# First cross attention of a six-stage kernel: output product from rounded parts and rests, and loads and first products in another order

## What is computed

```python
def _L0_xattn_ref(latents, context, ln_l_w, ln_l_b, ln_c_w, ln_c_b, Wq, Wkv, Wo, bo):
    H, D = 16, 64                    # INNER = 1024
    lat = layernorm(latents, ln_l_w, ln_l_b)
    ctx = layernorm(context, ln_c_w, ln_c_b)
    q = (lat @ Wq).reshape(b, n, H, D).transpose(0, 2, 1, 3)
    k, v = jnp.split(ctx @ Wkv, 2, axis=-1)
    ...
    attn = jnp.clip(jnp.einsum('bhnd,bhsd->bhns', q, k) * D ** (-0.5), -11.0, 11.0)
    attn = jax.nn.softmax(attn, axis=-1)
    out = jnp.einsum('bhns,bhsd->bhnd', attn, v)
    return out.transpose(0, 2, 1, 3).reshape(b, n, INNER) @ Wo + bo

x = x + _L0_xattn_ref(_layernorm(x, axis=-1), ctx_1024, ...)     # x (16, 64, 256), ctx (16, 256, 256)
x = x + _L0_attn_ref(_layernorm(x, axis=-1), ...)                # and four stages more
```

## Time and profile before

| | us |
|---|---|
| median of 3 runs | 1001.87 |
| lowest, highest | 1000.32, 1002.91 |
| the profiled execution | 1002.35 |
| its span, first to last instruction | 1000.6 |
| TensorE busy in the span | 953.0 (95%) |
| VectorE, ScalarE, GpSimd busy | 612.9, 446.0, 169.0 |
| mean granted clock of TensorE | 0.986 of 2.4 GHz |

### The profile page before, as it was taken

The page is one execution under the profiler, slowest core; times in us unless marked ns, Lnnn a source line. Parts: engine busy times, 40 slices in busy tenths (PEclk is TensorE's granted clock), DMA queues, the critical chain, the costliest instruction groups (busy, mean ns, idle before and its releaser), DMA issues.

```text
span 1000.6 us, 25932 instructions
## 1 busy us (share of the span) xinstructions
PE 953.0 (95%) x10693; PEld 818.4 (82%) x10693; DVE 612.9 (61%) x1448; ACT 446.0 (45%) x893; POOL 169.0 (17%) x357
## 2 busy tenths in 40 slices
PE   5999999999999989999989999997999999999998
PEld 4788888888888777887779999995888887877887
DVE  5655754654532655667798787776787863554242
ACT  3333332333332466654236666653444343673241
POOL 2312212112012212334310000013112000110000
PEclk9999999999999999999999999997999999999999
DMA  9443142132110292000059999962312002000000
GB/s 323 129 106 75 33 106 74 33 85 52 35 40 4 80 382 85 3 12 24 23 157 343 377 356 360 307 131 46 54 35 44 3 3 75 3 2 1 11 11 22
DMA packets 158612, 101.16 MB, mean 101 GB/s; under 512 B 102104, under 2 KB 148128, under 8 KB 157984
## 3 DMA queue, kind: packets, MB, share of 16 engines
q1 hardware_dynamic: 156960, 95.31, 31.9%
q0 software_dynamic: 1536, 4.20, 1.3%
HBM read 82.96 MB, written 16.52 MB: 99 GB/s over the span
## 4 chain that ended last, share of the span: by engine, by line
PE 82%; DVE 9%; ACT 5%; issue 2%; DMA 1%; POOL 0%; SPq 0%; DVEq 0%; ACTq 0%; POOLq 0%
PE ps L642 9%; PE ps L657 8%; PE ps L2374 8%; PE ps L2387 6%; PE ps L2710 6%; PE ps L674 3%; PE ps L1488 3%; PE ps L1195 3%; PE ps L596 3%; PE ps L693 2%; PE ps L1585 2%; PE ps L626 2%; PE ps L1120 2%; PE ps L1527 2%; PE ps L1130 2%; PE ps L1569 2%
## 5 line engine op out<-in xcount | busy, mean ns | idle before, releaser
L2374 PE MATMUL ps<-moe_xT,ew 128*128 128x128 f32 x736 | 89.5, 275 | 0.9 <-issue 0.8
L785 ACT ACTIVATE x0pT<-ps 128x512 f32<-128x512 f32 x64 | 38.2, 598 | 110.9 <-PE ps L657 110.9
L2374 PEld LDWEIGHTS ps<-moe_xT,ew 128*128 128x128 f32 x736 | 85.8, 192 | 1.7 <-issue 1.4
L1029 POOL TENSOR_SCALAR x0pT<-x0pT 128x512 f32<-128x512 f32 x64 | 40.3, 630 | 188.1 <-ACT x0pT L785 187.1
L2710 PE MATMUL ps<-f,ffw 128*128 128x512 f32 x256 | 60.7, 398 | 0.8 <-issue 0.6
L2710 PEld LDWEIGHTS ps<-f,ffw 128*128 128x128 f32 x256 | 48.9, 192 | 12.0 <-issue 0.9
L2387 PE MATMUL ps<-ew_2hi,eh_hi 128*128 128x256 f32 x184 | 55.5, 301 | 3.2 <-DVE eh_lo L2513 2.8
L642 PE MATMUL ps<-x0wv_hi,x0cT_hi 128*128 128x512 f32 x128 | 53.2, 416 | 4.2 <-DVE x0A_lo L915 4.2
L2323 DVE TENSOR_TENSOR ew_2lo<-ew,ew_2hi 128x1024 fp32r<-128x1024 f32 x46 | 55.9, 1216 | 0.0
L2570 POOL DMA_INDIRECT yg<-moe_out,slot x16 | 16.3, 1017 | 232.2 <-DMA moe_out<-moe_y 162.1
L657 PE MATMUL ps<-x0A_hi,x0cT_hi 128*128 128x512 f32 x128 | 52.0, 406 | 2.5 <-ACT x0pT L785 2.5
(11 more groups left out here) (337 smaller groups left out, 2428.7 us busy)
## 6 DMA issues: line engine op xcount, KB each, us to landing
ew<-L_ffn_W_dram SPq DMA_DIRECT2D x46, 1024.0 KB, 7.7
x0cin<-ctx_dram SPq DMA_DIRECT2D x8, 512.0 KB, 4.7
x1cin<-ctx_dram SPq DMA_DIRECT2D x64, 64.0 KB
x0cn_rows<-x0cn SPq DMA_DIRECT2D x7, 512.0 KB, 2.8
x0cn_blocks<-x0cn_rows SPq DMA_DIRECT2D x56, 64.0 KB, 2.4
x0att_rows<-x0att SPq DMA_DIRECT2D x14, 256.0 KB, 2.5
x0att_blocks<-x0att_rows SPq DMA_DIRECT2D x56, 64.0 KB, 2.6
moe_out<-moe_y SPq DMA_DIRECT2D x23, 128.0 KB, 4.3
```

What stands on the lines that cost most here:

```text
L785: nc.scalar.activation(g.pT[:, u, :], ps[:, S_BANK[u % 2], :], ACT.Exp, scale=64.0 ** -0.5).then_inc(C0.exp, 1)
L1029: nc.gpsimd.tensor_scalar(g.pT[:, u, :], g.pT[:, u, :], high, low, ALU.min, ALU.max).then_inc(C0.clip, 1)
L2374: last = nc.tensor.matmul(ps[:, n % 3, j * BT:j * BT + BT], ew1[b % NW][:, i, f * P:f * P + P], xT[b % 2][:, i, :], start=(i == 0), stop=( ...
```

## The change

*Output product.* `wo` is split once, in tile 0, into `wo_hi` (ScalarE, into the room of `w_sq[0]`) and `wo_lo` (VectorE, in place). The attention rows of each tile are split into `attT_hi` (ScalarE, into the second half of `padneg`) and `attT_lo` (VectorE, in place). A product of 8 float32 steps becomes one of 24 fp32r steps. It stands behind the eighth score group of the next tile, not between score groups 3 and 4; that of tile 6 stands in the next stage's list. `padneg` is set to zero again by GpSimd when x is done.

*Start.* TensorE begins with 18 products of zeros, then turns the K weights, then the latents, then the context. The latents are normalised ahead of the context rows. SP loads only the identity's 128 columns of the constants at first.

*Tile 0.* Turning the context of tile 1 moves behind v7 on VectorE and its scaling behind the last exponential on ScalarE.

*Loads.* The weights of the self attention and `wg` are loaded behind tile 0's attention rows, those of `w_sq[0]` when x is done.

The diff, cut to its core:

```diff
-        def ln_rstd_pool(pool, k, idx):
+        def ln_rstd_pool(pool, k, idx, first=0):
+            c = slice(first, first + k)
...
-            FILLS += [(("x0", t - 1), "y")] * (t > 0) + [(("x0", t + 1), "lat")] * nxt
-            FILLS += [(("x0", t), f"v{i}") for i in range(4, 8)]
+            FILLS += [(("x0", t + 1), "lat")] * nxt
+            FILLS += [(("x0", t), f"v{i}") for i in range(4, 8)] + [(("x0", t - 1), "y")] * (0 < t < T - 1)
             if nxt:
...
+            def out_products(t, what, ks):
+                for k in ks:
+                    for n, (m, w) in enumerate(((g.attT_hi, g.wo_hi), (g.attT_hi, g.wo_lo), (g.attT_lo, g.wo_hi))):
+                        last = nc.tensor.matmul(bank_of(t, what)[:, 0:D], m[:, k, :], w[:, k, :], start=(k == ks[0] and n == 0), stop=(k == ks[-1] and n == 2))
+                last.then_inc(C0.fill, 1)
+
             def fill_y(t):
...
-                pe.wait_ge(C0.attT, 2 * t + 2)
+                    pe.wait_ge(C0.w_lo, KD + 4)
...
+            pe.wait_ge(C0.zeros_lat_ones, 1)
+            for _ in range(18):
+                nc.tensor.matmul(ps[:, S_BANK[0], 0:P], g.pT[:, 0, 0:P], g.pT[:, 0, 0:P], start=True, stop=True, skip_group_check=True)
+            pe.wait_ge(ld["const"], 32)
+            for i in range(4):
+                fill_K(i)
+            fill_lat(0)
             fill_cT(0, 0)
...
-                if t > 0:
-                    fill_y(t - 1)
                 if nxt:
...
+                if 0 < t < T - 1:
+                    fill_y(t - 1)
...
+            def attT_upper(t):
+                act.wait_ge(C0.attT, 4 * t + 2)
+                if t > 0:
+                    wait_filled(act, t - 1, "y")
+                for pg in range(2):
+                    nc.scalar.activation(g.attT_hi[:, 4 * pg:4 * pg + 4, :], g.attT[:, 4 * pg:4 * pg + 4, :], ACT.Copy).then_inc(C0.attT_hi, 1)
+
+            def attT_upper_last(pg):
+                wait_filled(act, T - 1, f"T{pg}")
+                nc.scalar.activation(g.attT_hi[:, 4 * pg:4 * pg + 4, :], bank_of(T - 1, f"T{pg}").rearrange("p (c n) -> p c n", c=4), ACT.Copy).then_inc(C0.attT_hi, 1)
+
+            def wo_upper(i):
+                if i == 0:
+                    act.wait_ge(ld["x0o"], 16)
+                nc.scalar.activation(g.wo_hi[:, 2 * i:2 * i + 2, :], g.wo[:, 2 * i:2 * i + 2, :], ACT.Copy).then_inc(C0.w_hi, 1)
...
+            K(0)
+            K(1)
+            K(2)
+            lat(0)
             cT(0)
-            K(0)
-            lat(0)
-            K(2)
...
+                if nxt and t > 0:
+                    cT(t + 1)
                 if nxt:
-                    cT(t + 1)
...
+                if t > 0:
+                    attT_upper(t - 1)
+                if t == 0:
+                    wo_upper(0)
+                    wo_upper(1)
                 v(t, 6)
                 exp(t, 6)
                 exp(t, 7)
+                if t == 0:
+                    cT(1)
+                    wo_upper(2)
+                    wo_upper(3)
...
+            def attT_lower(t, pg):
+                dve.wait_ge(C0.attT_hi, 2 * t + pg + 1)
+                half = slice(4 * pg, 4 * pg + 4)
+                nc.vector.tensor_tensor(g.attT_lo[:, half, :], g.attT[:, half, :], g.attT_hi[:, half, :].bitcast(F32), ALU.subtract).then_inc(C0.attT, 1)
...
+            def norm_first():
+                dve.wait_ge(ln_rstd, 1)
+                nc.vector.tensor_scalar(g.lat[:, :], x[:, 0, :], ln_mv[:, 4, 0:1], ln_rs[:, 4:5], ALU.subtract, ALU.mult).then_inc(C0.zeros_lat_ones, 1)
+                dve.sem_inc(dve_go, 1)
+                dve.wait_ge(C0.zeros_lat_ones, 2)
+                nc.vector.bn_stats(g.ln_st[:, 4, :], g.lat[:, :]).then_inc(ln_stats, 1)
+                dve.wait_ge(ln_stats, 2)
+                dve.sem_inc(dve_go, 1)
+                nc.vector.bn_aggr(ln_mv[:, 4, :], g.ln_st[:, 4, :]).then_inc(ln_aggr, 1)
+                for k in range(4):
+                    last = nc.vector.tensor_scalar(g.cn[:, k, :], g.cin[:, 0, k, :], ln_mv[:, k, 0:1], ln_rs[:, k:k + 1], ALU.subtract, ALU.mult)
+                last.then_inc(ln_done, 1)
+                dve.wait_ge(ln_rstd, 2)
+                nc.vector.tensor_scalar(g.lat[:, :], g.lat[:, :], ln_mv[:, 4, 0:1], ln_rs[:, 4:5], ALU.subtract, ALU.mult).then_inc(ln_done, 1)
+
+            nc.vector.memset(g.pT[:, 0, 0:P], 0.0).then_inc(C0.zeros_lat_ones, 1)
...
-                if nxt:
+                if nxt and t > 0:
                     turn_context(t + 1)
+                if t > 0:
+                    v(t, 3)
+                if nxt and t > 0:
+                    cT(t + 1)
+                    cT_split(t + 1)
+                if more:
+                    norm(t + 2, 1)
                 if t > 0:
                     turn_att(t - 1, 0)
                     turn_att(t - 1, 1)
-                    v(t, 3)
-                if nxt:
-                    cT(t + 1)
-                    cT_split(t + 1)
-                if t > 0:
-                    residual(t - 1)
-                if more:
-                    norm(t + 2, 1)
                 v(t, 5)
                 if more:
                     norm(t + 2, 2)
+                if t > 0:
+                    attT_lower(t - 1, 0)
+                    attT_lower(t - 1, 1)
                 v(t, 7)
+                if 0 < t < T - 1:
+                    residual(t - 1)
                 if more:
                     norm(t + 2, 3)
+                if t == 0:
+                    turn_context(1)
+                    cT(1)
+                    wo_lower(0)
                 attend(t, 0)
+                if t == 0:
+                    cT_split(1)
                 if nxt:
                     q(t + 1)
+                if t == 0:
+                    wo_lower(1)
+                    wo_lower(2)
+                    wo_lower(3)
+                if nxt:
                     A_lower(t + 1, 0)
                     A_lower(t + 1, 1)
                     attend(t, 1)
@@ -1018,7 +1093,7 @@
                     v(t + 1, 1)
                 if t == 1:
                     self_tables(dve)
-            return attend, attT, add_y, residual
+            return attend, attT_lower_last, add_y, residual
 
         def pool_x0(pool):
...
+                x0_y(T - 2)
...
+                x0_residual(T - 2)
+                x0_attT(0)
...
-            whole(cst[:, :], a["consts"], ld["const"])
+            whole(ident, a["consts"][:, C_IDENT:C_IDENT + P], ld["const"])
...
+            whole(cst[:, P:C_ALL], a["consts"][:, P:C_ALL], ld["rest"])
...
+                if t == 2:
+                    for i, w in enumerate(("wq", "wkv")):
+                        whole(w_mla[:, :, 64 * i:64 * i + 64], weight("L0_attn_" + w), ld["mla"])
+                    for i, w in enumerate(("wqr", "wqr_swapped", "wkr", "wkr_swapped")):
+                        whole(w_mla[:, :, P + P * i:2 * P + P * i], weight("L0_attn_" + w), ld["mla"])
+                    whole(w_mlao[:, :, :], weight("L0_attn_wo"), ld["mla"])
+                    sp.wait_ge(pool_setup, 4)
+                    whole(w_mlac[0:64, 0:P], a["L0_attn_wqc"], ld["mla"])
+                    whole(w_mlac[64:P, P:2 * P], a["L0_attn_wkc"], ld["mla"])
+                    whole(w_mlac[64:P, 2 * P:2 * P + D], a["L0_attn_wv"], ld["mla"])
+                    whole(wg[:, :, 0:E], weight("L0_ffn_Wg"), ld["wg"])
             sp.wait_ge(C0.x_done, T)
+            for i, w in enumerate(("Wq", "Wk", "Wv", "Wo")):
+                whole(w_sq[0][:, :, i, :], weight("L0_ffn_" + w), ld["sq0"])
             for i, w in enumerate("QKVO"):
...
+            nc.gpsimd.memset(padneg[:, B // 2:B, :], 0.0).then_inc(pool_setup, 1)
```

More of the change, by code:

```diff
@@ L1857, in act_self @@
                 hT(lo)
-                last(T - 1)
+                last(0)
                 lat(lo)
@@ L1861, in act_self @@
                 rope(lo)
+                last(1)
                 hT(lo + 1)
@@ L2969, in _ @@
         def _(pe):
-            pe.wait_ge(ld["const"], 32)
             x0 = pe_x0(pe)
```

107 lines of the change are left out of this document (48 added, 59 removed).

## The result

| kernel | median us | lowest to highest | executions |
|---|---|---|---|
| before | 1001.10 | 1000.30 to 1002.91 | 4 |
| after | 989.05 | 986.92 to 989.54 | 4 |

The medians differ by 12.05 us, 1.2%. The ratio estimated from all executions is 0.9865, with a 95% interval of 0.9837 to 0.9893, which is 10.7 to 16.3 us. The profiled execution of after took 989.54 us, its span is 987.8; before's were 1002.35 and 1000.6. The forecast was 991.0.

The account below looks back on a forecast made before the run. TensorE was taken as the bound, 82% of the span. Output products 4.3, tile 7's halves 0.4, tile 0's stall 4.0, first output product 0.7 and start 1.4 sum to 10.8 us off, median 991.0, range 987.0 to 996.0.

Parts of the forecast that it names:

- Output product: Tiles 0 to 6: 24 fp32r products at 0.118 us take 2.84 us for 3.46, saving 4.3 us together.
- The 216 ns a pair: Output product: counter-estimate with unhidden weight loads, 24 pairs in 5.2 us, longer than now; the prediction did not follow it.
- Its operands: ScalarE's copies (1.2 us a tile) and VectorE's subtractions (1.4) hide behind their waits for TensorE; cost 0.
- The halves: Tile 7's two half output products go from 1.73 to 1.42 us each, 0.6 together, taken at 0.4.
- GpSimd's memset: Zeroing half of padneg when x is done, half of 3.52 us, nothing of the chain behind it; cost 0.
- Tile 0's stall: TensorE's 2.48 us wait and the slow clock's 1.54 us go as tile 1's context moves; 4.0 us, bounds 1.5 to 4.0.
- The 0.7 of the first output product: Its 0.5 us wait goes as it stands some 13 us later, and its 3.69 us become the others', 0.2 more.
- The start: wk lands near 9.2, zeros end near 6.5, the first v product comes earlier; 1.4 us, bounds 0 and 2.2.
- rival (a): The start gives nothing (slow wk transposes or another load lasts): 992.4, or 992.5 to 994 with tile 0 waits; chance 0.22.
- The gain of the order: At the start, latents' normalisation ends near 11.9 for 12.83, cT_hi comes at 14.0 to 15.1 for 15.95; no separate size.
- Rival (c): The 4.2 us of v products' waits for A's evictions go as well, giving 987; chance 0.07.
- Rival (d): Attention rows late for their output product in every tile, 4.0 us each: 1007 (four tiles) to 1019 (seven); chance 0.03.

Follow-up runs that it names:

- y_fp32: The changed kernel with its output products in float32 again, without rounded parts and rests, at their new places; 994.94 us.
- y_twice: The changed kernel with each of the 24 output products of tiles 0 to 6 issued twice, the copy into the bank's unused half; 1010.04 us.
- zeros_30: The changed kernel with 30 products of zeros at the start, not 18; 987.94 us.
- best: The changed kernel with the next tile's first score group ahead of its second v product, 30 zero products, and q(0)'s copy between wv's two roundings; 985.98 us.
- after_again: The changed kernel once more, unaltered, in another group of runs; 989.46 us, ratio to before 0.9901.
- before_late: The kernel before with only tile 1's context turned, scaled and split behind v(0,7) and attend(0,0), plus the SyncE wait this needs; 995.97 us.
- turn_early: The changed kernel with the turning, scaling and split of tile 1's context at their old places in tile 0's lists; 997.03 us.
- const_whole: The changed kernel with the whole table of constants (297 KB) loaded ahead of wk again in place of the identity's 64 KB; 989.63 us.
- score_first: The changed kernel with the first score group of tile t+1 ahead of its second v product; 987.93 us, its profiled execution disturbed (2316.21 us).
- no_zeros: The changed kernel without its 18 products of zeros at the start; 991.43 us.
- score_first2: Second run of the changed kernel with the first score group of tile t+1 ahead of its second v product; 984.18 us.

## Why the prediction was right

- **Output product.** 24 products in 2.83 us (forecast 2.84) and a half in 1.42 (1.42). y_fp32 gives 3.46 back, y_twice shows the loads hidden. Right in mechanism and size: the sum had it from the row of twelve in the expert layer, not from the weight load's length. The 216 ns a pair that the prediction set against it was an estimate that added load and product. The Trainium skill (TensorE: Matmul & The Clock Gate, Back-to-back issue gap) says that the spacing is set by both, but pipelined, and has no figure for such pairs at 256 columns. The measured 0.118 us decides.
- **Its operands.** ScalarE's and VectorE's extra work was costed at 0, and no new wait of TensorE between 22 and 310 us shows, the first A rest of tile 1 included. The next stage's rope rotation was forecast near 318 and begins at 317.28. The halves were taken at 0.4. Their own rows are 0.63 us shorter, and 0.49 of that is left at sa_max.
- **GpSimd's memset.** "With nothing of the chain behind it. Cost 0" was wrong. By the timelines it cost 0.7 us: VectorE's two operations were slower beside GpSimd's work, and h is on the chain. In the same place y_fp32, zeros_30, best and after_again have 0.86 to 1.00 and 0.88 for the two operations; before_late, which lacks the memset, has 0.61 and 0.40. No run took the memset out of the changed kernel, so its part is read from these timelines, not from an experiment. The Trainium skill (SBUF — State Buffer, SBUF: two separate sides) has a rule that may lie behind it: VectorE and GpSimd share a pair of ports, and whichever takes it first holds it for its whole instruction. On VectorE's side the rule names only an operation in a two-port mode, or one with two SBUF inputs beside a GpSimd operation that reads SBUF. The rows fit such a wait, but no run shows which mode the two operations ran in, so the mechanism is not shown. The forecast looked only at who waits for the memset's result, not at what GpSimd's queue then runs beside.
- **Tile 0's stall.** 4.0 forecast, 4.16 in after, 4.14 in before_late, where nothing else of the change is. The stall is of the place in the two queues. turn_early made it 6.5: a stall's size depends on when its rows come and on how long the slow clock lasts behind it, and is not a constant of the place.
- **The 0.7 of the first output product.** Its size is right, its cause is not. The prediction gave it to the product's later place; before_late has all of it with the product where it was. With tile 1's context moved, the attention rows come in time for the old place too.
- **The start.** 1.4 forecast, 1.31 in the profiled execution. The steps were wrong, though, and made up for one another. wk was to land at 9.2 by its bytes and landed at 10.1 (const_whole: bytes don't decide it). The zeros were to end near 6.5 and ended at 7.5, so that the gap of 2.7 us came out as forecast from two terms that were each 1 us off. And the forecast weighed "fast or slow" as one unknown of the kernel, rival (a); it is one of each execution, slow in five of eight. In the forecast's own terms, rival (a) nearly holds in the slow executions. The gain of the order, which the forecast derived from the latents' and cT_hi's earlier times, shows as 0 to 0.3 at the slow pace. What was not seen at all is that at the fast pace the chain comes through wv's landing and ScalarE's queue (0.8 us for q's copy).
- **Rival (c)** was that the 4.2 us of waits go as well. They stayed, as said. score_first shows that they go with one score product moved, for 3.9 us.
- **Rival (d)**, a late output product in every tile, is not there: tiles 1 to 7 have one period of 38.10.
- **The total.** The region gave 10.7 for 10.8, and that two misses nearly cancel in it is luck: 0.4 more at the handover to the next stage, and 0.8 less where the memset stands. At the handover before's chain goes through ScalarE for 0.95 us (its last exponential and sa_hT, 324.75 to 325.70), and after's stays on TensorE, with tile 6's product in that place. The median fell by 12. The surplus is the slow spell that before had at 700 to 710 us and after did not, 1.2, and 0.9 in the last stores, whose cause was not looked for. Neither is the change's doing as far as the runs show. after_again's ratio, 0.9901, is 9.9 us (7.3 to 12.6), and its median lies 11.3 us under that of before beside it.

## What to carry to other kernels

Price a product by a row of the same form in the same trace; the length of its weight load says nothing where loads are hidden. A step that is early in an in-order queue and late in its data costs its wait, the slow clock behind it, and what the delay upsets after that, so move it behind the work that is ready; here four moved calls gave 4.8 of the 12 us, as the trace of before_late has it. And where an engine waits 0.5 us in every tile for a copy of its own last product, put a product that doesn't need it in between: that one move was worth 3.5 us by the means and 3.9 by the traces, about a third of what the whole change gave.

## What the runs showed of the hardware

**The clock falls while TensorE is busy without a break.** TensorE by stretches of 10 us, of after (us, busy and instructions of PE, PEld, DVE, ACT, POOL, granted clock, DMA share, GB/s):

```profile
750.00:760.00 10.00, 10.00 (x130) 7.90 (x130) 7.20 (x17) 4.26 (x8) 2.51 (x5) 0.85 0.05 13
...
900.00:910.00 10.00, 10.00 (x38) 8.15 (x39) 2.11 (x5) 1.66 (x3) 0.86 (x3) 0.84 0.00 1
```

and of before:

```profile
700.00:710.00 10.00, 10.00 (x198) 8.41 (x197) 6.21 (x9) 3.01 (x5) 0.00 (x0) 0.84 0.34 54
```

A mean of 0.83 to 0.85 over 10 us is 3.0 to 3.4 us at the lower of the two levels, 1.2 GHz. In these three stretches the trace has TensorE busy all the while. Each of the thirteen traces has one to three such spells behind 700 us, at other places each time: before at 700, 760 and 910, after at 750 and 900, after_again at 710, near 770 and at 900, best at 740 only. (Before's at 910 and after_again's at 900 have some 0.6 us of idle time in their 10 us.) y_twice, no_zeros, const_whole and score_first2 have one more between 340 and 380 us. By the clock each costs up to 1.5 to 1.7 us, and best, with one, has the shortest span. What sets them off is open. The times of one kernel go with them: of after_again's six executions, those with a mean clock of 0.991 have spans of 986.0 to 986.5 us, and that with 0.981 has 993.7. So a gain of 1 us is to be read between two landmarks of a trace, not from totals.

**The same gap does not always cost the clock.** At the start, idle times of 1.85, 2.70 and 2.87 us left TensorE at its fast pace, and 1.96, 1.99 and 2.62 us did not.

**VectorE slows beside GpSimd.** Two small operations took 0.17 and 0.41 us with GpSimd idle and 0.86 and 0.88 beside its memsets and its additions. In before, the first took 0.62 us beside additions alone.

**Fewer bytes in short rows landed no earlier.** 64 KB in rows of 512 B ahead of wk in place of 297 KB in long ones: wk in at 10.18 and 10.17 us, with the queues at 351 and 383 GB/s. Over thirteen traces wk took 7.0 to 8.5 us behind the short rows and 7.0 to 7.2 behind the long ones.
